# Attention with a post-LayerNorm block: operands of the attention kept as scaled half-precision pairs, weights in two buffers

## The reference, cut to what matters

```python
# x: (2, 512, 512) float32; 32 query heads, 8 key/value heads, head size 128
q, k, v = x @ Wq, x @ Wk, x @ Wv                  # k, v shared by 4 query heads
scores = where(causal, q @ k.T * 128**-0.5, -inf)
x = layernorm(x + (softmax(scores) @ v) @ Wo)
base = x @ W_base.T + b_base
w = sparsemax(x @ W_router.T + b_router)          # 8 experts
x = layernorm(x + base + sum_e w_e * (x @ A_e) @ B_e)
```

## Time and profile before

| | |
|---|---|
| median of 3 runs | 771.97 us (771.06 to 772.99) |
| profiled execution | 771.9 us, span 770.1 us |
| PE busy | 725.7 us, 94% |
| DVE, ACT, POOL busy | 510.8, 434.3, 138.2 us |
| chain that ended last | PE 51%, DVE 19%, ACT 18%, issue 8% |

### The profile page before, as it was taken

The page is one execution under the profiler, slowest core; times in us unless marked ns, Lnnn a source line. Parts: engine busy times, 40 slices in busy tenths (PEclk is TensorE's granted clock), DMA queues, the critical chain, the costliest instruction groups (busy, mean ns, idle before and its releaser), DMA issues.

```text
span 770.1 us, 10813 instructions
## 1 busy us (share of the span) xinstructions
PE 725.7 (94%) x3552; PEld 569.9 (74%) x3552; DVE 510.8 (66%) x1466; ACT 434.3 (56%) x1070; POOL 138.2 (18%) x149
## 2 busy tenths in 40 slices
PE   8788999999999999999999999999999999978996
PEld 6676777777787777877777777877777877655774
DVE  4657666666757666576667666576666675677776
ACT  4465655575565655665656655665556556564222
POOL 3111300220021300220021300220021201251333
PEclk9999999999999999999999999999999999989998
DMA  7525523553435424553336334454436253462301
GB/s 218 165 42 111 121 42 70 129 118 68 77 89 118 117 46 78 137 110 69 69 83 139 94 67 75 120 109 69 69 95 145 49 97 96 91 129 41 69 29 68
DMA packets 200775, 71.76 MB, mean 93 GB/s; under 512 B 169744, under 2 KB 192784, under 8 KB 200720
## 3 DMA queue, kind: packets, MB, share of 16 engines
q1 hardware_dynamic: 200720, 71.08, 42.4%
HBM read 27.02 MB, written 2.10 MB: 38 GB/s over the span
## 4 chain that ended last, share of the span: by engine, by line
PE 51%; DVE 19%; ACT 18%; issue 8%; POOL 2%; DMA 2%; SPq 0%; DVEq 0%; POOLq 0%; ACTq 0%
PE bank L951 14%; PE bank L1007 13%; PE bank L996 8%; DVE p L829 8%; PE bank L973 6%; ACT p L684 6%; ACT pr L674 5%; DVE pr L794 4%; PE bank L962 4%; ACT oT_hi L691 2%; PE bank L1038 2%; ACT wo_hi L647 2%; POOL wq_lo L595 1%; ACT qT L659 1%; PE bank L938 1%
## 5 line engine op out<-in xcount | busy, mean ns | idle before, releaser
L674 ACT ACTIVATE pr<-pr,mx 128x128 f32<-128x128 f32 (+3 forms) x256 | 142.6, 557 | 173.7 <-DVE mx L794 148.6
L684 ACT ACTIVATE p<-pr,ri 128x128 f16<-128x128 f32 (+3 forms) x256 | 129.1, 551 | 96.9 <-DVE ri L820 93.7
L829 DVE SCALAR_TENSOR_TENSOR p<-pr,ri,p 128x128 f16<-128x128 f32 (+3 forms) x256 | 140.2, 589 | 28.0 <-ACT p L684 27.9
L973 PE MATMUL bank<-kT,qT 128*128 128x256 f32 (+2 forms) x576 | 139.9, 356 | 7.4 <-DVE mx L794 6.8
L973 PEld LDWEIGHTS bank<-kT,qT 128*128 128x128 f32 x576 | 101.5, 191 | 30.3 <-DVE mx L794 9.7
L996 PE MATMUL bank<-pT,v 128*128 128x512 f16 x480 | 119.8, 381 | 1.3 <-DMA pT<-p 1.3
L1007 PE MATMUL bank<-wo_hi,oT_hi 128*128 128x512 f32 x256 | 108.3, 423 | 5.3 <-DVE oT_lo L835 5.3
L951 PE MATMUL bank<-xT_hi,wq_hi 128*128 128x512 f32 x256 | 101.7, 397 | 9.1 <-POOL wq_lo L595 8.9
L794 DVE CUSTOM_DVE_ANT_0 pr<-bank,mask 128x256 f32<-128x256 f32 (+2 forms) x192 | 103.3, 549 | 5.6 <-PE bank L973 4.4
L738 DVE TENSOR_TENSOR qT<-bank,qT 128x512 fp32r<-128x512 f32 x64 | 44.1, 689 | 94.0 <-ACT qT L659 94.0
L1007 PE MATMUL bank<-wo_lo,oT_hi 128*128 128x512 f32 x256 | 102.1, 399 | 0.0
(11 more groups left out here) (129 smaller groups left out, 1071.8 us busy)
## 6 DMA issues: line engine op xcount, KB each, us to landing
raw<-in_wo SPq DMA_DIRECT2D x32, 256.0 KB, 3.3
raw<-in_wq SPq DMA_DIRECT2D x28, 256.0 KB, 3.7
raw<-in_wk SPq DMA_DIRECT2D x8, 256.0 KB, 3.6
raw<-in_wv SPq DMA_DIRECT2D x8, 256.0 KB, 3.5
y<-in_x SPq DMA_DIRECT2D x1, 2048.0 KB, 10.4
pT<-p SPq DMA_TRANSPOSE x128, 3.7
out<-y SPq DMA_DIRECT2D x8, 256.0 KB, 2.0
raw<-in_xT SPq DMA_DIRECT2D x4, 256.0 KB, 4.8
```

Source lines behind the costliest of these rows:

```text
L674: eng.activation(pr[:, h, 0:w], pr[:, h, 0:w], ACT.Exp, bias=mx[:, k:k + 1], scale=-1.0, accum_out=rs[:, k:k + 1]).then_inc(sems["exp"], 1)
L684: eng.activation(halves_of_probs(t, h)[0], pr[:, h, 0:w], ACT.Copy, scale=ri[:, 1, k:k + 1]).then_inc(sems["p_hi"], 1)
L829: made = eng.scalar_tensor_tensor(out=lo, in0=pr[:, h, 0:w], scalar=ri[:, 1, k:k + 1], in1=hi, op0=ALU.mult, op1=ALU.subtract)
L973: made = eng.matmul(out, qTs[:, u % 2, q, h, i * 128:(i + 1) * 128], kTs[:, u % 2, k, 0:w], start=q + k == 0, stop=q == 1)
```

## The change

Every operand of the attention becomes a pair of half-precision (float16) terms: x, wq, wk, wv, wo, q, k, the attention output. Half precision has a small range, so each tensor is first multiplied by a power of two made from its own largest magnitude: `most` (DVE, over the float32 data in the staging buffer: 2048 columns for wq and wo of a head, 512 for wk, 1024 for wv), then `turn` (PE turns the row maxima; DVE makes the factors and the products that undo them), then `spread` (PE and DVE). `turn` and `spread` take the place of `vt` and `vb`; they come once for each head, at tile i = 0 of the unit before (i = 1 for the first). The undoing factors go into the scale of `max` and into the addition to y.

POOL multiplies a piece in place by its factor, ACT then makes the high part from the scaled piece, and POOL the low part. At the start some pieces go over ACT and DVE alone. The pieces of head n = g + 1 are split in unit (g, 0): wq 0 and wk at i = 1, wq 1 to 3 at i = 2, wv (for n = 1, 3, 5) with wo 0 and 1 at i = 3, and wo 2 and 3 at i = 0 of unit (g, 1). The wq, wk and wo buffers are doubled, and a head's raw weights are fetched one head earlier. The last part keeps fp32r, with buffers of its own. At the start, wq is fetched by ACT's queue ahead of the rest, and the high parts of x wait for the factors.

```diff
+            return {0: [("wo", n, 2), ("wo", n, 3)]}.get(i, [])
...
+        return {1: [("wq", n, 0), ("wk", n)], 2: [("wq", n, h) for h in (1, 2, 3)],
+                3: more + [("wo", n, 0), ("wo", n, 1)]}.get(i, [])
...
+        if b == 0 and g + 1 < G and i == (g == 0):
+            fill[4:4] = most_of_set(g + 1)[2] + [("turn", g + 1)]
+            fill += [("spread", g + 1)]
...
+        if u and splits(u, i):
+            fill[3:3] = splits(u, i)
...
+        if b and i > 1 and g + 2 < G:
+            yield from most_of_set(g + 2)[i - 2]
...
+        wk = sb("wk", [128, 2, 2, 512], f16)
+        wo = sb("wo", [128, 2, 2, HG, 512], f16)
+        kT = sb("kT", [128, 2, 2, 512], f16)
+        qT = sb("qT", [128, 2, 2, HG, 512], f16)
...
                 elif name in PIECES and not on_dve(name, key):
                     hi, lo = halves(name, key)
+                    scale = scale_for(name, key)
+                    if scale:
+                        pool.wait_ge(*done(f"raw{pieces[(name, *key)]}", name, *key))
+                        pool.wait_ge(*done("scales", scale[1]))
+                        eng.tensor_scalar(raw_of(name, key), raw_of(name, key), scale[0], None,
+                                          ALU.mult).then_inc(sems["scaled"], 1)
+                        pool.wait_ge(*done("scaled", name, *key))
                     pool.wait_ge(*done("hi", name, *key))
-                    eng.tensor_tensor(out=lo, in0=raw_of(name, key), in1=hi.bitcast(f32),
+                    eng.tensor_tensor(out=lo, in0=raw_of(name, key), in1=hi if scale else hi.bitcast(f32),
                                       op=ALU.subtract).then_inc(sems["lo_pool"], 1)
...
+                    act.wait_ge(*(done("scaled", name, *key) if scaled else done(f"raw{pieces[(name, *key)]}", name, *key)))
+                    if name == "wk" and key[0] >= 2:
+                        act.wait_ge(*done("K", 2 * key[0] - 3))
...
-                    eng.activation(qTs[:, u % 2, 0, h, :], psum("Q", u, h)[:, :], ACT.Copy).then_inc(sems["qT_hi"], 1)
+                    eng.activation(qT[:, u % 2, 0, h, :], psum("Q", u, h)[:, :], ACT.Copy, scale=DOWN).then_inc(sems["qT_hi"], 1)
...
+                elif name == "most":
+                    kind, n = key
+                    for piece in most_pieces(kind, n):
+                        dve.wait_ge(*done(f"raw{pieces[piece]}", *piece))
+                    c = maximum_column(kind, n, n if kind == "x0" else 0)
+                    eng.tensor_reduce(out=rowmax[:, c:c + 1], in_=most_input(kind, n), axis=mybir.AxisListType.X, op=ALU.max,
+                                      apply_absolute_value=True).then_inc(sems["most"], 1)
...
-                    eng.tensor_tensor(out=y[:, k, :], in0=psum("W", t)[:, :], in1=y[:, k, :], op=ALU.add).then_inc(sems["y"], 1)
+                    eng.scalar_tensor_tensor(out=y[:, k, :], in0=psum("W", t)[:, :], scalar=back_of[:, g, 2 + b:3 + b], in1=y[:, k, :],
+                                             op0=ALU.mult, op1=ALU.add).then_inc(sems["y"], 1)
```

More of the change, by code:

```diff
@@ L103, in plan @@
     for piece in first:
         yield ("fetch", *piece)
+    yield ("consts",)
     yield ("rows",)
-    yield from first[0:6]
+    yield ("most", "k", 0)
+    yield ("most", "x0", 0)
+    yield ("most", "x0", 1)
+    yield ("most", "x0", 2)
     yield ("warm",)
+    yield ("turn", "A")
+    yield ("most", "q", 0)
+    yield ("spread", "A")
+    yield ("wk", 0)
+    yield ("x", 0, 0)
+    yield ("x", 0, 1)
+    yield ("x", 0, 2)
+    yield ("x", 0, 3)
     yield ("K", 0)
+    yield ("turn", "B")
@@ L136, in plan @@
-    yield ("vt", 0)
+    yield ("Vp", 0, 0)
+    yield ("x", 1, 2)
+    yield ("x", 1, 3)
     yield ("inv", 0, 1)
     yield ("norm", 0, 1)
-    yield ("Q", 1, 1)
-    yield ("vb", 0)
+    yield ("Vp", 0, 1)
     yield ("rest", 0, 1)
-    yield ("Vp", 0, 0)
-    yield ("wo", 0, 0)
-    yield ("wo", 0, 1)
-    yield from ahead(1, shares([("Vp", 0, 1), ("wo", 0, 2), ("Vp", 0, 2), ("wo", 0, 3), ("Vp", 0, 3)], 6))
+    yield ("turn", "D")
+    yield ("Q", 1, 0)
+    yield ("spread", "D")
+    for h in range(HG):
+        yield ("fetch", "wq", 1, h)
@@ L146, in plan @@
+    yield ("fetch", "wk", 1)
+    yield from ahead(1, shares([("Vp", 0, 2), ("wo", 0, 0), ("K", 1), ("wo", 0, 1), ("Q", 1, 1), ("wo", 0, 2), ("Vp", 0, 3),
+                                ("wo", 0, 3)], 6))
     for t in range(NT):
@@ L647, in _ @@
-                    eng.activation(hi, raw_of(name, key), ACT.Copy).then_inc(sems["hi"], 1)
+                        for h in range(HG):
+                            act.wait_ge(*done("Q", NU - 1, h))
+                    if scale and not scaled:
+                        act.wait_ge(*done("scales", scale[1]))
+                        made = eng.activation(hi, raw_of(name, key), ACT.Copy, scale=scale[0])
+                    else:
+                        made = eng.activation(hi, raw_of(name, key), ACT.Copy)
```

442 lines of the change are left out of this document (258 added, 184 removed).

## The result

The changed kernel takes 958.5 us (median of 4 runs, 956.8 to 960.0), the kernel before in the same session 771.9 (771.1 to 773.0). The ratio is 1.242, 95% interval 1.239 to 1.244. The forecast was 835 with a range of 756 to 880: the kernel became slower, as forecast, but by 187 us and not by 63. The rival that came nearest, slower scaling on POOL with 870 to 885, had been given a chance of 0.07.

A forecast was written before the change was run, and what follows sets the result against it. PE's stream, busy for 725.7 of 770.1 us, was taken to set the time. The terms summed as 771.9 - 36 - 14 - 14 + 16 + 33 + 2 + 66 + 10 = 834.9, so 835 us, range 756 to 880.

The forecast's parts named there:

- largest term: ACT's high parts of weight pieces wait for POOL's subtraction and scaling, so PE waits for maxima: 66 us.
- slower scaling on POOL: Rival: POOL's scaling takes near 1.3 us and DVE is blocked beside it, 870 to 885 us; chance 0.07.
- PE's denser stream: On PE, half-precision products start closer together, 36 us gained, and the stall behind PV products goes, 14 us gained.
- waits that go: PE's waits for POOL's low part of wq (8.9 us) and behind `vt` (5 us) vanish: 14 us gained together.
- start: Before the first heads, factors and wq transfers delay Q to near 23 and tile 2's scores to near 59: 16 us lost.
- hand-over: Between POOL and ACT, each gap between high parts is 2.2 us, scaling taken as 0.7: 66 us lost, bounds 25 and 95.
- PE's distances: On PE, W products gain 0.019 us each and 2,050 others 0.011: 36 us gained, bounds nothing and 53.
- stall behind PV: The first fp32r product behind a PV product delays its successor 0.2 us, some 70 times: 14 us gained when gone.
- `most`, `turn`: At tile i = 0, PE's transposes wait 4.35 us for DVE's reductions: 33 us lost, plus 2 for wq's reduction.
- clock: After long waits PE runs at 1.2 GHz, losing 1.7 us a stretch, six counted: 10 us lost, bounds 0 and 27.
- What bounds the kernel: PE's stream sets the time; delays put into the DVE and ACT chain pass on until PE finds no score bank.
- The remainder beside POOL: DVE's remainders slow down beside POOL's instructions: 9 us if one in six added microseconds meets one, left to the upper end.

The follow-up runs named there:

- e1: The kernel before with only half-precision tiles for the operands, no maxima, factors, scaling or doubled weight buffers: 747.8 us, ratio 0.969.
- e8: The kernel before with half-precision tiles and the first wq piece of each next head fetched and split one tile earlier: 745.3 us, ratio 0.965.
- e7: The changed kernel, but POOL scales only 208 of the 512 columns of a piece: 927.5 us, ratio 1.201.
- e4: The changed kernel with ACT making high parts straight from the unscaled piece, and the turn and spread of the factors later in heads 2 to 7: 850.6 us, ratio 1.102.
- e5: e4 with the searches for maxima in heads 1 to 7 looking at only 64 columns: 805.0 us, ratio 1.044.
- e2: The changed kernel, but ACT makes the high part of every POOL piece from the unscaled raw piece, and POOL scales behind that: 855.7 us, ratio 1.109.
- e3: The changed kernel with PE's turn of the maxima moved behind two Q projections and the spread into the next tile, heads 2 to 7: 958.2 us, ratio 1.241.
- e6: The changed kernel with products that nobody reads added in heads 2 to 7 to keep PE busy in its waits: 949.5 us, ratio 1.229.
- e10: e4 with one single-column activation at the very start, so that ACT loads its function table early: 848.5 us, ratio 1.100.
- e16: e4 with unread products filling PE's waits up to the first spread of head 1: 846.9 us, ratio 1.097.
- e13: e4 with constants (4096) as the first set's factors, its searches, turns and spreads left out: 836.5 us, ratio 1.082.
- e12: e5 with a constant as the scale of the maxima instead of one read from memory: 800.5 us, ratio 1.037.

## Why the prediction was wrong, step by step

The mechanism of the largest term was right, and three sizes failed. PE's denser stream and the waits that go were credited with 64 us, and e1 gave 23.6: 14 were a stall that is not there, 14 were waits behind which others stand (e8), and most of the rest went into longer waits of the faster PE. The start was put at 16 us and is some 35. In the hand-over the term "I take 0.7" for POOL's scaling failed: it takes 1.58 us, and 0.757 us of it are worth 31 (e7).

| step | forecast | measured |
|---|---|---|
| PE's distances | -36 | -37 in PE's busy time; -24 in the end (e1) |
| stall behind PV | -14 | 0 (e1, and before's own rows) |
| waits that go | -14 | 0 in the six heads, -2.5 in all (e8, for wq's wait alone) |
| start | +16 | +39 to tile 8 (e4 against e1), with 4 that stood under `turn` |
| `most`, `turn` | +33 and +2 | +45.6 for the searches (e5 against e4); PE's place open |
| hand-over | +66 | +103 to 108 (e2; e3 against e4), the clock behind it within |
| clock | +10 | +9 or more (e6), not to be added to it |
| not in the sum | | 20 in the six heads (e5 against e1) |

From kernel to kernel the times go without overlap: 771.4 before, -23.6 (e1), +102.8 (e4), +107.9 (after). The forecast had 64 of gain, 51 and 76 for the same three, so it missed 40, 52 and 32.

**What bounds the kernel: right as far as it went.** "A delay put into that chain is not swallowed" holds for what ACT, POOL and DVE were given. But the same sentence holds for gains, and the prediction let PE keep all of its own. PE's distances were priced to a microsecond (36 and 37), in part by luck: the 0.011 us for the 2,050 products beside W was taken because over half of them were thought narrower than 512 columns. Only 896 are, and the gain is 0.011 to 0.012 at every width (0.227 to 0.216, 0.175 to 0.163, 0.120 to 0.109). And 10 of the 37 went into waits for wq, maxima and transfers. The removed waits went the same way: with wq's 13.0 us gone, that for the transfers rose by 9.3 (e8). PE at 94% was paced in part by what it waited for.

**The stall behind PV: wrong in its reading.** The prediction took one long distance and not the short one ahead of it.

**The hand-over: right in mechanism, wrong in one size.** The order of scale, high, low, scale makes ACT wait in every gap, and e2, whose one edit is that order, gives 103 us back. The term that failed is "I take 0.7": the scaling takes 1.58 us, more than the subtraction (1.16, with a half-precision result; before 1.36), and lies outside the bounds of 0.53 and 1.36. As the subtraction got shorter, the gap is 2.88 us and not 2.2. The prediction's sum done again with 2.88 gives some 94 us in place of 66. (It gives 93 for the stated upper bound too, a gap of 2.86, where the text has 95.) With its 10 for the clock that would be 104, against 102.8 (e2) and 107.6 (e3 against e4). The Trainium skill (GPSIMD Engine Reference, Elementwise — side-by-side cycle accounting) gives 0.769 us as the measured best case of a loop over 512 elements. Here the measurement, 1.58, differs and decides.

**`most` and `turn`: near in size, not shown in cause.** PE waited as forecast before the transposes of each head in the kernel after:

```profile
410.79 0.27 PE L1173 MATMUL bank<-ident,rowmax 128*1 128x128 f32 x1 [0.92 <-DVE mx L947]
415.68 0.59 PE L1173 MATMUL bank<-ident,rowmax 128*1 128x128 f32 x2 [4.62 <-DVE rowmax L884]
```

The second wait is 4.62 us against the 4.35 forecast. e3 takes this wait away, but a wait for a score bank takes its place, so the record does not say what the wait alone costs. What it does show is the searches: 45.6 us where 35 were put down. The prediction's sum has wo's and wk's in full, with wv's, and 0.3 us a head for wq's, 2 in all. Its 33 also hold the addition to y and the hand-overs, so that 35 comes near 45.6 is partly luck.

**The start: too small by some 19 us.** Q began at 29.1, not 23, and the scores of tile 2 came at 74.8, not 59. The walk took up K at the lower clock (3.59 us for eight products) and ACT's table load (1.28) nowhere, and both lie on the path to Q: K begins 1.3 us earlier in e10, and eight products take 2.19 us in e16. 15 us of the whole are the factors' chain (e13), as thought. Head 1's searches and turn fall into head 0. The sum had 2 us for two searches there and some 4 for the turn; tiles 3 to 4 took 17 us more than before even in e13.

**The clock: right in its number, not in its count.** Half-clock time was 199 us in the whole trace and not the 20 of six stretches. But when e6 took 97 of them away, only 9 us came back, because the helpers catch up where PE is slow, as the prediction said. That 10 and 9 agree is luck, since the count was far too small and the fills themselves may have cost up to 7.

**The remainder beside POOL** was left to the upper end with 9 us. In the kernel after, the remainders of the probabilities (256 of them) take 0.579 us on average, before 0.589: nothing. It appears in e4 with 0.621, 11 us in all. There 73 of them lie for over half of their time beside an instruction of POOL, in the kernel after 39. Those of 384 columns take 0.80 us beside POOL and 0.61 otherwise. The Trainium skill (GPSIMD Engine Reference, Specifications) says that the two engines share their interfaces to SBUF, with contention for instructions of two SBUF inputs; by that rule, e4 agrees.

## What to carry to other kernels

Price a new instruction that stands in a repeated hand-over by the slowest row of its engine and not between two faster ones, and take a bound above that row: here 0.76 us in one instruction was 31 us in the kernel. Where two engines work on a piece in turn (scale, copy, subtract), let the one that others wait for read the raw piece, as in e2, which gave back 103 us with two lines. Before moving an instruction out of a wait, ask which buffer it holds and until when: e3 removed a wait of 4.6 us a head and made one as long for the bank that it kept. And when one engine gets faster, count its gain only as far as the others leave it: 37 us of PE's time were 24 of the kernel's.

## What the runs showed of the hardware

- POOL's product of a 128 x 512 tile by a factor per partition, in place, takes 1.58 us (74 times, after), more than its subtraction of two such tiles (1.16). Over 208 columns it takes 0.83 (e7).
- Where a W product in fp32r follows a half-precision PV product (30 times in the kernel before), its start stands 0.19 us early in the record, and the next start 0.19 us late against it; the two cancel.
- Fp32r products of 512 columns start 0.227 to 0.234 us apart (medians by line, kernel before), half-precision ones 0.216.
- `max` with its scale read from memory takes 0.743 us for 512 columns (after), with a constant 0.681 (e12; 64 each).
- DVE's remainders of 512 columns take 1.08 us where they lie for over half of their time beside an instruction of POOL (16 times in e4), 0.75 otherwise (48 times).
- Bringing the granted clock from 0.91 to 0.99 over 642 us was worth 11 us, at most some 18 (e6). The slow stretches of this kernel stand behind waits.
